# Attention scores turned in whole 128x128 transposes, and exponentials by half of the heads

## The reference, cut to what matters

```python
scores = jnp.einsum('bhqd,bhkd->bhqk', q, k) / jnp.sqrt(jnp.float32(HD))
scores = scores * mask - 10000.0 * (1.0 - mask)
probs = jax.nn.softmax(scores, axis=-1)
return jnp.einsum('bhqk,bhkd->bhqd', probs, v)
```

## Time and profile before

| | us |
|---|---|
| median of 3 runs | 1089.6 |
| lowest, highest | 1088.24, 1089.82 |
| profiled execution, span from the first to the last instruction | 1086.8 |
| PE, DVE, ACT, POOL busy | 1004.1, 988.4, 849.4, 681.9 |
| matmul records of line 584 (`prob_turn`) | 2048 |
| granted TensorE clock, mean | 0.983 |

### The profile page before, as it was taken

One profiled execution on the slowest core, in us unless ns is written; L12 is line 12 of the kernel. 1 busy time (PEld: TensorE's weight loads), 2 busy tenths in 40 slices (PEclk: granted clock), 3 DMA queues, 4 the chain that ended last, 5 costly groups with the idle time before them and its releaser, 6 DMA issues.

```text
span 1086.8 us, 46478 instructions
## 1 busy us (share of the span) xinstructions
PE 1004.1 (92%) x19180; PEld 890.8 (82%) x19180; DVE 988.4 (91%) x2328; ACT 849.4 (78%) x1905; POOL 681.9 (63%) x909
## 2 busy tenths in 40 slices
PE   6776989999999999999999999999999999998997
PEld 5665778888888888888888888888888888886786
DVE  4989897999999999999999999999999999988763
ACT  3446789887888888888788888878888888786894
POOL 3777575666666667666667676666676676655221
PEclk9879999999999999999999999999999999999999
DMA  8843112222322222222222222222222222311111
GB/s 275 280 114 74 42 39 41 44 45 58 59 49 51 52 57 43 49 54 58 58 49 45 57 47 48 50 58 58 49 49 54 56 44 49 61 37 37 31 37 36
DMA packets 169700, 67.70 MB, mean 62 GB/s; under 512 B 151184, under 2 KB 167312, under 8 KB 168464
## 3 DMA queue, kind: packets, MB, share of 16 engines
q1 hardware_dynamic: 169488, 64.72, 26.1%
HBM read 26.93 MB, written 4.19 MB: 29 GB/s over the span
## 4 chain that ended last, share of the span: by engine, by line
PE 37%; ACT 26%; DVE 20%; issue 11%; POOL 4%; DMA 2%; SPq 0%; ACTq 0%; POOLq 0%; DVEq 0%
PE psum L457 9%; PE psum L598 7%; PE psum L630 7%; ACT staging L2017 7%; PE psum L470 6%; ACT hid_mlp L2017 6%; PE psum L564 3%; ACT L2003 3%; PE psum L584 3%; DVE mx_lat L1248 3%; ACT L2017 2%; ACT probT_self L2003 2%; DVE late L1267 2%; DVE mx_ctx L1254 2%; DMA turned_mlp<-pair_mlp 1%
## 5 line engine op out<-in xcount | busy, mean ns | idle before, releaser
L2499 POOL TENSOR_TENSOR prob_self<-prob_self,add_self 128x512 f32<-128x512 f32 x64 | 86.8, 1376 | 66.1 <-DVE prob_self L1238 63.4
L2499 POOL TENSOR_TENSOR prob_cross<-prob_cross,add_cross 128x512 f32<-128x512 f32 x64 | 94.5, 1495 | 52.9 <-DVE prob_cross L1238 52.9
L2505 POOL TENSOR_TENSOR late<-late,mx_ctx 128x512 f32<-128x512 f32 x64 | 67.3, 1053 | 86.6 <-DVE mx_ctx L1254 84.1
L2017 ACT ACTIVATE hid_mlp<-psum,folded,undo_in 128x128 f32<-128x128 f32 x256 | 95.6, 455 | 6.9 <-PE psum L457 6.4
L2017 ACT ACTIVATE staging<-psum,cols,undo_in 128x128 f32<-128x128 f32 x256 | 97.4, 481 | 3.3 <-PE psum L457 3.1
L457 PE MATMUL psum<-turned_mlp,hi_n 128*128 128x128 f16 x1024 | 94.2, 221 | 1.6 <-DVE late L1267 1.0
L630 PE MATMUL psum<-hi_n,staging 128*128 128x256 f16 x512 | 94.3, 273 | 1.5 <-DVE staging L1297 1.5
L457 PE MATMUL psum<-turned_mlp,hi_m 128*128 128x128 f16 x1024 | 93.4, 220 | 0.6 <-DMA turned_mlp<-pair_mlp 0.5
L630 PE MATMUL psum<-hi_m,parts_mlp 128*128 128x256 f16 x512 | 89.9, 273 | 1.2 <-DVE xb L1291 0.9
L457 PE MATMUL psum<-turned_mlp,lo_n 128*128 128x128 f16 x512 | 90.3, 221 | 0.0
L457 PE MATMUL psum<-turned_mlp,lo_m 128*128 128x128 f16 x512 | 89.6, 220 | 0.0
(11 more groups left out here) (265 smaller groups left out, 3850.0 us busy)
## 6 DMA issues: line engine op xcount, KB each, us to landing
xin<-in_x SPq DMA_DIRECT2D x32, 128.0 KB, 2.2
late<-in_ctxT SPq DMA_DIRECT2D x4, 1024.0 KB, 5.7
ctxT<-in_ctxT SPq DMA_DIRECT2D x32, 128.0 KB, 2.0
late<-in_x SPq DMA_DIRECT2D x4, 1024.0 KB, 5.6
out<-xb SPq DMA_DIRECT2D x32, 128.0 KB, 1.9
staging<-in_w_m SPq DMA_DIRECT2D x2, 1024.0 KB, 7.2
staging<-in_w_n SPq DMA_DIRECT2D x2, 1024.0 KB, 5.2
mask<-in_mask_cross SPq DMA_DIRECT2D x32, 32.0 KB, 2.0
```

Of the source, the lines that this page charges most:

```text
L2017: last = e.activation(hid[t][g][:, j * P:(j + 1) * P], ps[:, j * P:(j + 1) * P], ACT.Gelu_apprx_tanh, bias=b1[:, 4 * g + j:4 * g + j + 1], ...
L2499: e.tensor_tensor(ch, ch, over_heads(a[:, :]), ALU.add).then_inc(sem["added_" + t], 1)
L2505: e.tensor_tensor(ch, ch, over_keys(max_of("ctx", h)), ALU.subtract).then_inc(sem["shifted_ctx"], 1)
```

## The change

The turn is made over both batches: each transpose takes all 128 partitions (both batches' queries) by 128 columns (two heads by 64 keys), so there are eight a set, four a half, and half `h` goes to bank `h`. The turn of a half waits for the shift of that half only and signals by itself. Exponentials go by half. `mix` picks its 64 columns, batch `a`, out of 128. `masked` and the shift of lat wait for the turn of their own half in the unit before.

```diff
@@ -268,8 +268,8 @@
         passing = [late[:, 4 * i:4 * i + 4, :].rearrange("p c n -> p (c n)") for i in range(2)]
         prob = {t: [sb(f"prob_{t}{h}", [P, 512]) for h in range(2)] for t in ("self", "cross")}
         prob |= {t: [late[:, 2 * i + h, :] for h in range(2)] for i, t in enumerate(("ctx", "lat"))}
-        probT = {t: [sb(f"probT_{t}{a}", [P, NP, S]) for a in range(BU)] for t in ("self", "cross")}
-        probT |= {t: [late[:, 4 + 2 * i + a, :].rearrange("p (n k) -> p n k", n=NP) for a in range(BU)] for i, t in enumerate(("ctx", "lat"))}
+        probT = {t: [sb(f"probT_{t}{h}", [P, NP // CHUNKS, P]) for h in range(CHUNKS)] for t in ("self", "cross")}
+        probT |= {t: [late[:, 4 + 2 * i + h, :].rearrange("p (n k) -> p n k", n=NP // CHUNKS) for h in range(CHUNKS)] for i, t in enumerate(("ctx", "lat"))}
         hid = {"mlp0": [sb(f"hid_mlp0{g}", [P, 512]) for g in range(2)], "mlp1": [staging[:, g, :] for g in range(2)]}
         parts = {"mlp0": [sb(f"parts_mlp0{g}", [P, 512]) for g in range(2)], "mlp1": [staging[:, 2 + g, :] for g in range(2)]}
         part = {t: [a[:, :].bitcast(F16) for a in parts[t]] for t in parts}
@@ -574,16 +574,14 @@
             def prob_turn(u, t, b):
 
                 q.wait_ge("constants", IDENT)
-                q.wait_ge("shifted_" + t, 2 * u + 2)
-                claim(b, ("prob_turn", t, 1, u), "probT_" + t, 2 * u + 2)
                 for h in range(CHUNKS):
-                    for j in range(4):
-                        n = 4 * h + j
-                        for a in range(BU):
-                            here = slice(S * a, S * a + S)
-                            last = e.transpose(bank[in_bank["prob_turn", t, a, u]][:, n * S:(n + 1) * S],
-                                               prob[t][h][here, j * P:(j + 1) * P], ident[here, here])
-                last.then_inc(sem["prob_turn_" + t], 1)
+                    q.wait_ge("shifted_" + t, 2 * u + h + 1)
+                    if h == 1:
+                        claim(b, ("prob_turn", t, 1, u), "probT_" + t, 2 * u + 2)
+                    for j in range(NP // CHUNKS):
+                        last = e.transpose(bank[in_bank["prob_turn", t, h, u]][:, j * P:(j + 1) * P],
+                                           prob[t][h][:, j * P:(j + 1) * P], ident[:, :])
+                    last.then_inc(sem["prob_turn_" + t], 1)
 
             @of_unit
             def mix(u, t, b):
@@ -595,7 +593,7 @@
                 for j, p in enumerate(PAIRS[0] + PAIRS[1]):
                     for n, s in enumerate(sets):
                         for a in range(BU):
-                            last = e.matmul(ps[S * a:S * a + S, p * VW:(p + 1) * VW], probT[s][a][:, j, :], val[s][:, a, p, :],
+                            last = e.matmul(ps[S * a:S * a + S, p * VW:(p + 1) * VW], probT[s][j // 4][:, j % 4, S * a:S * a + S], val[s][:, a, p, :],
                                             start=(n == 0), stop=(n == len(sets) - 1))
                 last.then_inc(sem["mix_" + t], 1)
 
@@ -1223,7 +1221,7 @@
             @of_unit
             def masked(u, t, h):
                 q.wait_ge("score_" + t, u + 1)
-                q.wait_ge("prob_turn_" + t, u)
+                q.wait_ge("prob_turn_" + t, 2 * (u - 1) + h + 1)
                 ps, ch = scores(t, h, u), in_tiles(prob[t][h][:, :])
                 if t == "ctx":
                     q.wait_ge("squared_part", 2 * SCANNED)
@@ -1258,7 +1256,7 @@
                 if t == "lat":
                     q.wait_ge("max_both", 2 * u + h + 1)
                     q.wait_ge("squared_part", 2 * SCANNED)
-                    q.wait_ge("prob_turn_lat", u)
+                    q.wait_ge("prob_turn_lat", 2 * (u - 1) + h + 1)
                     src, top = scores("lat", h, u), max_of("ctx", h)
                 else:
                     q.wait_ge("max_" + t, 2 * u + h + 1)
@@ -1996,11 +1994,11 @@
                 last.then_inc(sem["val_" + t], 1)
 
             @of_unit
-            def exponential(u, t, a):
-                src = bank[in_bank["prob_turn", t, a, u]][:, :].rearrange("p (n t) -> p n t", n=NP)
-                q.wait_ge("prob_turn_" + t, u + 1)
+            def exponential(u, t, h):
+                src = bank[in_bank["prob_turn", t, h, u]][:, :].rearrange("p (n t) -> p n t", n=NP // CHUNKS)
+                q.wait_ge("prob_turn_" + t, 2 * u + h + 1)
                 q.wait_ge("mix_" + ("lat" if t == "ctx" else t), u)
-                e.activation(probT[t][a][:, :, :], src, ACT.Exp).then_inc(sem["probT_" + t], 1)
+                e.activation(probT[t][h][:, :, :], src, ACT.Exp).then_inc(sem["probT_" + t], 1)
 
             @of_unit
             def gelu(u, t, g):
```

## The result

The changed kernel takes 1095.05 us (median of 7 runs, 1091.95 to 1096.62), the kernel before on the same chip 1089.82 us (7 runs, 1088.0 to 1091.63). The median lies 0.05 us from the forecast of 1095.0 and inside its range.

The account below looks back on a forecast made before the run. The loop was taken as bound by a ring through DVE, PE and ACT. Span 1086.8 + 5.4 (loop +4.2, fill and tail +1.2) + 2.8 outside the span = 1095.0 us; 8-in-10 range 1083.5 to 1099.5.

Parts of the forecast that it names:

- Price of a whole transpose: PE's 128x128 f32 transpose: 0.109 us likeliest, at two f16 columns per f32 column; lower bound 0.056 to 0.064.
- Rivals 1 and 3: 1: whole transposes stream at f16's pace, 1084.1 us, chance 0.17; 3: their load isn't hidden, about 1130 us, chance 0.03.
- Step 1: Lat and ctx turns: four transposes (0.44 us) covered by idle time, twelve after the wait; +0.17 us on the ring.
- the ring: Loop body's cycle: DVE's lat shift, PE's turns to `q_cross`, ACT to self exponentials, PE's self mix, DVE again; 30.78 us.
- Steps 2 to 4: Self turn +0.13, cross turn +0.23, less 0.30 slack on PE's way; ways meet at self mix, +0.23 us a pass.
- PE's way: Path through PE's self and cross turns to the self mix, beside the ACT way; 0.30 us slack; +0.23 us forecast.
- Step 4: Self mix, where both ways meet: the later counts, +0.23 us a pass; DVE's `denominators` wait grows from 0.25 to 0.5.
- Step 5: About every third pass, PE waits for the DMA before `hidden` mlp0: +0.17 is swallowed, +0.06 us is left.
- Fill and tail: Outside the loop: splitting gains some 0.6 us, longer turns cost +0.6; guessed +1.2 us, between -3 and +4.
- Rival 2: A wash: halves save more outside the loop or the ring has more slack; about 1090 us, chance 0.15.

Follow-up runs that it names:

- run 5: Changed kernel with the self scores' eight whole transposes made twice in every pass; 1116.91 us, ratio 1.0251.
- run 2: Changed kernel, but both halves of a turn wait for both shifts; 1108.9 us, ratio 1.0165.
- run 4: Changed kernel with ctx and lat turned as before the change, with one wait for both shifts; 1092.52 us, ratio 1.0016.
- run 8: Kernel before, small transposes kept, with run 7's bank swap and the wait parted by half for ctx and lat only, from the loop on; 1086.25 us, ratio 0.9965.
- runs 6 and 9: 6: kernel before, small transposes kept, wait parted by half for all sets, with run 7's bank swap; 1086.92 us, ratio 0.9975. 9: see run 9.
- run 9: Run 8 with the loop's ctx turn in bank 4 for 2 and self projection in 2 for 4; 1086.98 us, ratio 0.9974.
- run 7: Kernel before with only a bank swap in the loop: lat turn in 6 for 4, projections of self and cross in 4 and 6; 1088.88 us, ratio 0.9997.

## Why the prediction was right

The time, the sign and the pass are as forecast; some of the ways to them are not. That the median came within 0.05 us is luck: runs of one kernel spread by several us, and errors in the sum cancel, as said below.

- **Price of a whole transpose**: 0.109 us, record 272 ns forecast; 0.109 to 0.110 and 273 ns measured, and run 5 priced eight of them at 0.87 us. The changeover of 0.10 us against f16 went, and stayed ahead of the mix. Self turn 0.87 forecast, 0.88 measured, cross 0.97 and 0.96. Right.
- **The Trainium skill's rule.** The moving side ran at two f16 columns per f32 column, and the forecast of 272 ns held. A transpose leaves one such record where an ordinary f32 matmul leaves two, so on the moving side it is twice as fast. The load of a whole f32 transpose took 141 ns against 192 for an ordinary f32 load, but it is hidden. "TensorE: Matmul & The Clock Gate", section Terms, of the Trainium skill gives four times the speed for FP32 in the transpose mode; the trace agrees with it neither on the moving side, at 2, nor on the load, at 192/141 = 1.4. Rivals 1 and 3 are out.
- **Step 1** (cover of half 0, 0.44 us): run 2 measured 0.50. Right within 0.06. The rest of it, +0.17 on the ring, came out at +0.13 at the end of the turns and +0.12 at the addition (first two columns of the table). The cover was the larger by these 0.06; mis-sized by 0.05.
- **Steps 2 to 4** (self and cross, +0.06 on PE's way beyond its slack of 0.30): run 4 gave +0.06, all of it behind the addition (22.94 to 23.00), where after has the same. Right. Both steps together I put at +0.23; it is +0.18, and the 0.05 is that of step 1.
- **Step 4, DVE's wait** at `denominators` of self (0.5 us a pass, 12 in the stretch): wrong, 6.7. The step assumed that DVE meets PE only at the self mix. It meets it earlier, at the addition behind `project` self, with an idle time of 0.07 us that is too short for the list of waits. There DVE lost 0.12 of the 0.18, and run 2 confirms the place: 0.62 there (2.83 to 3.45), now long enough for the list, where it stands as 14.6 us in 24 times.
- **Step 5** (in the passes with the DMA +0.06 only): wrong, 31.19 against 31.01 is +0.18. What holds the DMA up is itself behind the turn by way of this addition (the chain of after goes from the turn over `project`, the addition, POOL and ACT into `pair_mlp` and the DMA), so these passes have no cover of their own. This is read from one such pass before and one after; the mean of all distances has grown by 0.18 too (30.84 to 31.02). Nor is it every third pass that takes 31.01 or more before, but 4 of 23. The 0.05 too much in most passes and the 0.12 too little in the others cancel: 24 passes were forecast at +4.2 us and came at +4.3. The agreement is better than the reasoning was.
- **Fill and tail** (+1.2, a guess): about +1 by the medians. The profiled executions can't check it, since their fills differ by more from run to run.
- **Rival 2** (a wash) is out: the ratio excludes it. Its argument, that DVE never waits long, was true and beside the point, for what counts is whether DVE waits, and where.

The change has thus two parts of opposite sign. A bank per half lets the turn start before the second shift, which is worth 0.50 us a pass with whole transposes; the whole transposes cost 0.87 us for eight where sixteen small ones, two at a time, took 0.74. Taking the first without the second, in banks that are free, gave 1086.25 us (run 8).

## What to carry to other kernels

A transpose over the full height streams 128 columns of the identity where a half-height one streams 64, and each f32 column costs the same, so where it replaces two half-height ones that run side by side (0.109 us against 0.064) it loses, here even with the change of shape beside f16 matmuls gone. A wait that is parted by halves does something only where no other wait of the same stage, a bank's release above all, ends at the same time: look at which events release the banks, and at the first instruction's start in the trace. And before pricing an earlier finish, measure how long its consumer really stands, also below the length that a list of waits shows: here that was 0.07 us, and of the 0.20 and 0.35 us by which the turns of runs 6 and 9 ended earlier the rest was worth nothing.

## What the runs showed of the hardware

- The same program of the fill ran at a mean granted clock of 1.00 in run 8 and of 0.83 in run 9 between 80 and 100 us, and its sixth `denominators` of self came at 174.6 and 179.9 us. These are not the only two courses: after and runs 2 and 4 had 0.91 there.
- Times of one kernel spread by up to 9.7 us (23 runs of the kernel before beside runs 8 and 9, 1087.21 to 1096.86), and the slow ones have the lower clock: the three fastest of them show a mean granted clock of 0.983, the three slowest 0.978, 0.972 and 0.969. This asks for many runs where 2 us matter.
- Exchanging the banks of three stages, without any other edit, shortened a pass by 0.09 us (run 7). The whole of it lies ahead of `score` ctx, which starts 0.29 us behind the last f16 matmul's start before and 0.20 in run 7. Before, it takes the bank of `project` self first and then that of `project` cross, which is released later; in run 7 it takes them in the other order, and its load shows the wait for the addition instead. Why that order of claims is cheaper was not tried further.
